# Decoder layer on one core: the start of the cross-attention placed within the second half of the self-attention

## The reference

```python
x = x + attn(layernorm(x), w_q, w_kv, w_dense)      # causal, 16 heads, 4 groups, head size 128
x = x + xattn(layernorm(x), ctx, mask, mask, Wq, bq, Wk, bk, Wv, bv)
x = x + ffn(layernorm(x), Wg, W1, W2, W3, bias)      # 8 experts, top 2

def xattn(target, source, target_mask, source_mask, ...):   # 16 heads of size 16, positions along the last axis (512)
    q = einsum('oc,bct->bot', Wq, target) + bq              # k, v from source in the same way
    dot = einsum('bhdt,bhds->bhts', q, k) / 4
    mask = target_mask[..., None] * source_mask[:, :, None, :]
    dot = mask * dot - (1 - mask) * 1e6
    amap = softmax(dot) * mask
    return einsum('bhts,bhds->bhdt', amap, v)
```

## Time and profile before

| | us |
|---|---|
| median of 3 runs | 2808.98 |
| lowest and highest | 2804.44, 2813.34 |
| the profiled execution, its time | 2802.59 |
| the profiled execution, its span | 2801.0 |
| PE busy in the span | 2603.9 (93%) |
| DVE busy | 1875.0 (67%) |
| ACT busy | 1455.1 (52%) |
| POOL busy | 995.5 (36%) |

### The profile page before, as it was taken

One profiled execution on the slowest core, in us unless ns is written; L12 is line 12 of the kernel. 1 busy time (PEld: TensorE's weight loads), 2 busy tenths in 40 slices (PEclk: granted clock), 3 DMA queues, 4 the chain that ended last, 5 costly groups with the idle time before them and its releaser, 6 DMA issues. The chain is left out here.

```text
span 2801.0 us, 51111 instructions
## 1 busy us (share of the span) xinstructions
PE 2603.9 (93%) x15536; PEld 1816.8 (65%) x15537; DVE 1875.0 (67%) x3845; ACT 1455.1 (52%) x2868; POOL 995.5 (36%) x1178
## 2 busy tenths in 40 slices
PE   7999999999999999999759999999999986399997
PEld 6888888888888888888524444444443423277775
DVE  6556655566544455554569898889888876576665
ACT  4334433345433344333337777777777765255554
POOL 1112211112111112211235665665665647433332
PEclk9999999999999999999879999999999988699999
DMA  4102222013201111111154555555655558655554
GB/s 150 69 7 75 75 75 75 26 49 136 91 31 61 45 45 60 60 47 43 53 123 118 133 136 136 139 131 136 139 135 130 133 147 287 230 101 106 111 106 83
DMA packets 140817, 282.49 MB, mean 101 GB/s; under 512 B 39344, under 2 KB 42288, under 8 KB 135616
## 3 DMA queue, kind: packets, MB, share of 16 engines
q1 hardware_dynamic: 112416, 214.99, 26.7%
q0 software_dynamic: 23664, 58.09, 10.0%
q10 hardware_dynamic: 4656, 8.40, 1.0%
HBM read 147.82 MB, written 81.68 MB: 82 GB/s over the span
## 5 line engine op out<-in xcount | busy, mean ns | idle before, releaser
L1566 DVE TENSOR_REDUCE b_negmax<-b_ps_s 128x2 f32<-128x1024 f32 x512 | 611.2, 1218 | 52.9 <-PE b_ps_s L1751 46.4
L278 POOL TENSOR_SCALAR probs<-probs,rinv 128x256 f32<-128x256 f32 x256 | 242.0, 945 | 1094.3 <-DVE rinv L435 1094.3
L1366 ACT ACTIVATE b_probs<-b_ps_s 128x1024 f32<-128x1024 f32 x512 | 520.0, 1020 | 198.9 <-PE b_ps_s L1762 197.6
L312 ACT ACTIVATE probs<-ps_s,negmax 128x128 f32<-128x128 f32 x256 | 94.1, 367 | 484.5 <-DVE negmax L428 484.5
L1775 PE MATMUL b_ps_o<-b_probs,b_v_stack 128*32 128x256 f32 (+1 forms) x2816 | 295.0, 491 | 0.9 <-ACT b_probs L1366 0.8
L1762 PEld LDWEIGHTS b_ps_s<-b_stack 56*128 56x128 f32 x1024 | 96.3, 184 | 272.4 <-issue 165.7
L1762 PE MATMUL b_ps_s<-b_stack 56*128 56x512 f32 x1024 | 257.6, 500 | 15.4 <-DVE b_negmax L1566 7.5
L1751 PE MATMUL b_ps_s<-b_stack 54*128 54x512 f32 x1024 | 228.7, 443 | 42.4 <-DMA b_stack<-b_split 24.0
L543 PE MATMUL ps_proj<-xT_h,wq_h 128*128 128x512 f32 x512 | 216.0, 422 | 0.0
L2461 POOL DMA_INDIRECT out<-e_y,e_place_int x71 | 118.1, 1664 | 253.4 <-DMA out<-e_y,e_place_int 218.4
L543 PE MATMUL ps_proj<-xT_h,wq_l 128*128 128x512 f32 x512 | 201.7, 394 | 0.0
(11 more groups left out here) (334 smaller groups left out, 6641.1 us busy)
## 6 DMA issues: line engine op xcount, KB each, us to landing
b_stack<-b_split SPq DMA_DIRECT2D x336, 128.0 KB
e_row<-rows_by_expert SPq DMA_DIRECT2D x71, 258.0 KB, 2.9
b_out_tiles<-row_sum_inverses SPq DMA_DIRECT2D x64, 256.0 KB
x<-acc SPq DMA_DIRECT2D x15, 1024.0 KB, 4.8
x_in<-in_x SPq DMA_DIRECT2D x8, 1024.0 KB, 8.1
normalised_x_split<-xT_h SPq DMA_DIRECT2D x8, 1024.0 KB, 9.8
normalised_x_split<-xT_l SPq DMA_DIRECT2D x8, 1024.0 KB, 11.0
acc<-in_x SPq DMA_DIRECT2D x8, 1024.0 KB, 11.3
```

What stands on the lines that cost most here:

```text
L278: nc.gpsimd.tensor_scalar(probs[:, s, P:3 * P], probs[:, s, P:3 * P], rinv[:, s, 1:2], None, ALU.mult).then_inc(probs_done, 1)
L312: nc.scalar.activation(probs[:, s, 0:P], ps_s[s][:, 0:P], ACT.Exp, bias=negmax[:, s, 0:1], accum_out=rowsum[:, s, 0:1])
L1366: nc.scalar.activation(probs[:, k % 2, p, :, :], ps[:], ACT.Exp, scale=0.25).then_inc(e_done, 1)
L1566: nc.vector.tensor_reduce(negmax[:, k, p, :], ps[:], AX.X, ALU.max, negate=True).then_inc(m_reduced, 1)
```

## The change

A new function `cross_preparation` allocates the cross-attention's weights, biases, `x_in`, `c_in`, `xn`, their splits and the small tensors at the addresses where they lie in the second phase, and returns one function per engine; `attention_phase` calls their parts. Its own tensors are laid out in another order, so that what lies under the prepared ones is not used any more at the time.

- SyncE: at the beginning of t = 8 it loads the mask cut into 128 rows of 64, the three weights and the biases; at the end of t = 8 it stores the mask rows in 32 transfers; at the beginning of t = 15 it loads sequence 0 (`x_in`, `c_in`, `mask_b`).
- GpSimd: `ident` and `minus_half` at the start; at t = 8, after each of the units 0 to 11, one step of the mask rows, now on 128 partitions; at t = 15 scale and shift after unit 6, and both low parts at the end.
- ScalarE, t = 15: high parts of the weights after units 1, 3, 5, normalised input after unit 8, its high part after unit 10, the context's high part after unit 14.
- VectorE, t = 15: low parts of the weights after units 2, 4, 6, statistics after unit 5. Its mask row operations are gone.
- The block of the self-attention doesn't wait for the last stores; SyncE waits for them before the first stack transfer, ScalarE before its first exponential.
- The cross-attention's block begins with the projections. SyncE issues the mask rows of quads 0 to 2 and sequence 1's load first, then waits for the tiles.

```diff
@@ attention_phase, sync @@
                 def body(t, kind, half):
+                    if kind == "fresh":
+                        load_weights_of_cross()
+                    if kind == "last":
+                        sp.wait_ge(proj_filled, FILLS * t + KT + G + 2)
+                        load_first_sequence()
...
+                    if kind == "fresh":
+                        store_mask_rows()
                 pairs(body)(sp)
-                sp.wait_ge(stored, 16 * (HALVES * PAIRS + TB))
@@ gpsimd @@
+                constants_of_cross()
...
+                        if kind == "fresh":
+                            mask_rows_step(u)
+                        if kind == "last" and u == TB + 2:
+                            norm_scale_of_cross()
+                    if kind == "last":
+                        pool.wait_ge(proj_filled, FILLS * (t + 1))
+                        lows_of_cross()
@@ scalar @@
+                        if last and u in (1, 3, 5):
+                            weight_high("kqv"[u // 2])
+                        if last and u == 8:
+                            first_normalised()
+                        if last and u == 10:
+                            first_x_high()
+                        if last and u == UNITS - 2:
+                            act.wait_ge(proj_filled, FILLS * (t + 1))
+                            first_context_high()
@@ vector @@
+                        if last and u in (2, 4, 6):
+                            weight_low("kqv"[u // 2 - 1])
+                        if last and u == 5:
+                            first_stats()
@@ cross_preparation (new) @@
+        def load_weights_of_cross():
+            sp.dma_start(mask_cut[:], mask.rearrange("b (c t) -> (b c) t", t=COLS)).then_inc(mask_loaded, 16)
+            for n, src in (("k", w_kT), ("q", w_qT), ("v", w_vT)):
+                sp.dma_start(w_stage[:, W_AT[n], :, :], src.rearrange("(k p) o -> p k o", p=P)).then_inc(w_loaded[n], 16)
+            load_bias("k", b_k)
+            load_bias("q", b_q)
+            sp.dma_start(bias_v[:], b_v.to_broadcast([P, C])).then_inc(bias_loaded["v"], 16)
+
+        def store_mask_rows():
+            sp.wait_ge(aux_step, AUX_STEPS)
+            for r in range(AUXROWS):
+                for side in range(2):
+                    for p in range(2):
+                        sp.dma_start(aux_dram[:, r, side, p, :].rearrange("b (c t) -> b c t", t=COLS), aux[:, r, side, :]).then_inc(aux_stored, 16)
...
+        def mask_rows_step(u):
+            if u == 0:
+                pool.wait_ge(mask_loaded, 16)
+                nc.gpsimd.memset(aux[:, AUXROWS - 2:AUXROWS, :, :], 1.0).then_inc(aux_step, 1)
+            if u == 1:
+                nc.gpsimd.tensor_scalar(one_minus[:], mask_cut[:], -1.0, 1.0, ALU.mult, ALU.add).then_inc(aux_step, 1)
+                pool.wait_ge(aux_step, 2)
...
+        def weight_high(name):
+            act.wait_ge(w_loaded[name], 16)
+            if name == "k":
+                act.wait_ge(aux_stored, 16 * 4 * AUXROWS)
...
+        def first_stats():
+            dve.wait_ge(xc_loaded, 32)
...
@@ cross_attention_phase, sync @@
-                sp.dma_start(mask_rows, mask).then_inc(mrow_loaded, 16)
-                load_weight("k", w_kT)
-                load_xc(0)
...
-                sp.wait_ge(aux_step, AUX_STEPS)
-                for p in range(2):
-                    sp.dma_start(aux_dram[:, 0:MASKROWS, :, p, :], aux).then_inc(aux_stored, 16)
-                    sp.dma_start(aux_dram[:, MASKROWS:AUXROWS, :, p, :], max_rows).then_inc(aux_stored, 16)
-                sp.wait_ge(aux_stored, 64)
+                sp.wait_ge(aux_stored, 16 * 4 * AUXROWS)
+                for q in range(QUADS - 1):
+                    stack_aux(0, q)
                 sp.wait_ge(xs_low, 1)
                 sp.wait_ge(cs_low, 1)
                 load_xc(1)
+                load_mask_col(0)
+                load_mask_r(0)
+                sp.wait_ge(x1_stored, 16 * X1_STORES)
                 sp.wait_ge(tile_low, 4)
-                stack_quad(0, 0)
-                stack_quad(0, 1)
+                stack_half(0, 0, 0, sp)
+                for i in range(2):
+                    stack_half(0, 1, i, sp)
```

More of the change, by code:

```diff
@@ L106, in attention_phase @@
         acc_loaded = sem("acc_loaded")
-        stored = sem("stored")
+        stored = ready["x1_stored"]
         stats_done = sem("stats_done")
@@ L721, in cross_attention_phase @@
+def cross_attention_phase(nc, x1_seq, context_seq, mask, mask_cols, aux_dram, rinv_dram, x2_seq, ready, tensors, prepared, prepared_small, W_PARTS, X1_STORES, route, size):
     B, C, T = x1_seq.shape
@@ L969, in stack_half @@
                                   half_stacked if (q, i) == (0, 1) else stacked[q], 16)
-        def load_bias(eng, n, src):
-            with nc.allow_non_contiguous_dma(reason="a small vector"):
-                heads = src.rearrange("(u d p i) h -> h u i d p", u=2, d=DH, p=2, i=2)
-                for q in range(QUADS):
-                    for i in range(2):
-                        eng.dma_start(bias[n][spread(q, i), :], heads[q // 2, q % 2, i]).then_inc(bias_loaded[n], 16)
-        W_AT = {"k": 0, "q": 1, "v": 2}
-        W_PARTS = {"k": 1, "q": 2, "v": 3}
         FIRST_BANKS = {"k0": ps_p[:], "k1": ps_s[0][:, 0, :], "q0": ps_s[0][:, 1, :], "q1": ps_s[1][:, 0, :],
@@ L2681, in decoder_layer, with cross @@
     xT_pairs = nc.dram_tensor("normalised_x_split", [B * S // BANK, 2, P, H // P, BANK], F32, kind="Internal").ap()
[L2682 to L2687 removed]
+    with ExitStack() as ctx:
+        ready, tensors, prepared, prepared_small, w_parts, prepare = cross_preparation(nc, ctx, x1, context, mask, x_wq, x_bq, x_wk, x_bk, x_wv, x_bv, aux)
+        attention_phase(nc, by_512(x), a_wq, a_wkv, a_wd, xT_pairs, by_512(x1), B * S, H, S, HEADS, GROUPS, ready, prepare)
+        x1_stores = 2 * (B * S // BANK) + BANK // P
+        def cross(route, size):
+            cross_attention_phase(nc, x1, context, mask, mask_cols, aux, rinv, x2, ready, tensors, prepared, prepared_small, w_parts, x1_stores, route, size)
+        context_and_experts_phase(nc, out, cross, f_wg, f_w13, f_w2, f_bias, *experts_scratch(nc))
 def kernel(**inputs):
```

343 lines of the change are left out of this document (194 added, 149 removed).

## The result

| | before | changed |
|---|---|---|
| median us | 2810.47 (4 runs, 2804.44 to 2813.34) | 2785.53 (4 runs, 2782.78 to 2786.92) |
| ratio, 95% interval | 1 | 0.9913 [0.9894, 0.9932] |
| the profiled execution, time and span | 2802.59, 2801.0 | 2785.0, 2783.5 |

The change saves 24.9 us of the median, 0.9%. A second comparison gave 2815.14 against 2787.72, 0.9911 [0.9878, 0.9944], so 27.4 us. The forecast was -26.7 us and 2782 us.

A forecast was written before the change was run, and what follows sets the result against it. TensorE's standstill at the handover was the limit, the phases otherwise keeping it supplied. Handover -32.5, t = 8 +1.3, last pair +4.5 give -26.7 us: 2782 against the median, range 2772 to 2796.

The forecast's parts named there:

- Step 1: Self-attention block's end: without the wait for the last store it ends at about 1374.9 against 1376.74, 1.8 us.
- The stack's landing: Handover: stack transfers took 6.1 us here, 3.9 in the next sequence; landing taken as 1391.0, bounds 1389.1 to 1391.3.
- Rival (d): Handover: DMA engines limit the starting stack transfers, shift only 20 us; -14 us, 2795, chance 0.06.
- I take 0, since the next item delays ScalarE by more than what is missing: t = 8: late dense weights stall ScalarE 0 to 2.7 us, taken as 0 because the mask's wait delays it more.
- cannot pass: t = 8: by ring order the mask's load stays behind the 1 MB store, so TensorE loses 1.3 us.
- Rival (e): After t = 8: 32 mask row stores block SyncE's queue; 83 us lost against 27 won, about 2865, chance 0.04.
- Last pair: Pair before the handover: added VectorE work costs 3.5 us and GpSimd's 1 us, sum 4.5, bounds 0 and 9.
- the lead of 1.3 us: Last pair: unit 3's probabilities are ready 1.3 us before being transposed, covering that much of VectorE's 4.8 us.
- each stall is at most 1.6 us: Last pair: added pieces are smaller and spread, so no TensorE stall exceeds 1.6 us and the clock may hold.
- rival (b): Last pair or mask's wait costs more, TensorE stalls over 2 us drop the clock; -17 to -22, about 2790, chance 0.14.
- GpSimd's low parts also move as a block and stay ahead of their readers: After the handover: sequence 1's low parts shift earlier with its other preparation and delay nothing; no cost entered.
- Rival (a): The forecast itself, whole kernel: -22 to -31 us, chance 0.62.

The follow-up runs named there:

- the run with all three improvements: Changed kernel with loads in t = 7 behind the accumulator's, GpSimd's low parts first, VectorE's additions behind its last unit; 2788.62 us, ratio 0.9890 to the kernel before.

## Why the prediction was right, and where its steps were not

**Handover: right in size, its parts less so.** 32.8 us against 32.5. Tiles ready 6.83 us after the first one, as taken over from the earlier trace rows. Step 1 was valued at 1.8 us; put back, the wait costs 3.3, since behind the longer pause TensorE's granted clock fell to 0.50 within the projections. The stack's landing was taken near the slower row, and it took 6.9 us. Rival (d), transfers limited by the DMA engines, did not happen in the changed kernel, but in the run in which VectorE takes two of the low parts the tiles were early and the product was not, so there the transfers bound what is left.

**t = 8: sum too small by 0.8 us, and the causes weighed wrongly.** Forecast +1.3, measured +2.14 and +2.04. The failing step is "I take 0, since the next item delays ScalarE by more than what is missing": the dense weights' lateness is 1.4 of the 2.0 us and the mask's wait 0.5 to 0.6. The mask's load, issued 0.42 us behind the 1 MB store, came 4.4 us later, at 728.2; the store had landed 4.7 us after its own issue, at 728.0. The Trainium skill (DMA: Bandwidth & Descriptors, Queues, rings and completion order) says that a DMA engine takes the descriptors of a ring in order, and the trace agrees; it also says that a later one may finish its write before an earlier one, so the forecast's "cannot pass" is more than the page states.

**Mask rows' stores: right.** The 32 issues took 22.62 us from 813.44, 0.7 us each, and t = 9 is no longer than before (82.75 us, where it was 83.06). Rival (e), 2865 us, is excluded.

**Last pair: the engine right, the sum right by luck.** Forecast +4.5, measured 4.7 in the first trace. But it was 3.5 for VectorE and 1 for GpSimd. GpSimd cost nothing that shows: no split was lengthened (1.26, 1.27 and 0.68 us), and scaling after scaling waits for VectorE, the one behind the normalisation too. VectorE's 4.7 us of work cost all they last, so the lead of 1.3 us saved nothing. The two errors cancel. The bound "each stall is at most 1.6 us" failed: one was 2.06 us, behind the statistics, though the clock stayed at 1.00 behind it, other than rival (b) has it for a stall over 2 us. Over all eight traces with these additions in the units, the pair took 64.4 to 67.0 us, 65.6 in the mean, so 5.8 us above before; five of them show a granted clock of 0.71 to 0.89 from 1370 to 1380 us, behind waits of 1.17 and 1.41 us that before has too. In the four variants with splits or all additions moved behind the last unit none does. That the additions make the fall likelier is what these counts suggest, not more. That VectorE gains no new lead from unit to unit is borne out: eight small pieces cost the same as four larger ones.

**After the handover: a step that was wrong.** "GpSimd's low parts also move as a block and stay ahead of their readers": they stay ahead of their readers, but they didn't move with the scores. GpSimd's low part of the input came 7.4 us later against the first product than before and fell on VectorE's copy of the maxima, 1.29 us instead of 0.18. The stretch grew by 0.9 to 1.3 us in the two traces of the changed kernel. With another order on GpSimd it is 27.68 to 28.18 us in four variants, against 28.61 to 29.77 in the traces with the old order and 27.70 before.

**Against the median.** -32.8 + 2.1 + 4.7 + 0.9 and +0.7 in other stretches of the attention part is -24.4 by the first pair of traces, without the sequences and the end. The medians say -24.9 and -27.4. Rival (a) it was. That 2782 is so near to 2785.5 is partly luck: the forecast had nothing for 0.9 us behind the handover and 0.8 us too little at t = 8, its two errors in the last pair cancel, and the conversion from trace to median was taken from one execution, 6.4 us below the median.

**Open.** From the last sequence's load to the end, the two traces of before take 653.1 and 653.5 us; the changed kernel and ten variants take 654.4 to 667.4. The code there is the same. Within it falls the start of the routing, where waits for transfers and for ScalarE (0.9 us in one trace, 15.0 in another) trade places. Both traces of before are of executions below its medians (2802.59 and 2805.91 us against 2810.47 to 2819.95), which speaks for luck. Whether the change costs some 3 us there, or before was lucky twice, these runs don't settle; nor whether the meetings of `b_r_out`, of which before shows none in two traces, became more frequent.

## To carry to other kernels

Work that is moved off a serial stretch is best put where its engine isn't part of a circle that sets the pace: here in the waits of 2 us at the tail, and a low busy share was no sign of such a place. Where engines turn at one pace, cutting the work into pieces saved nothing. Tiny transfers cost their issue time (0.64 us each here) to whatever is queued behind them, so they belong into a stretch in which the queue is idle. A wait at a block's end can cost more than it lasts, 3.3 us for 1.7 here.

## What the runs showed of the hardware

- An operation on 128x16 elements took 1.57 to 2.39 instead of 0.17 us when GpSimd's subtraction of 2.38 us had begun 0.02 to 0.85 us before it: `b_r_out` at 1524.65 ended with `p_x_l`, and in the run with all three improvements the value split took 2.51 instead of 0.68 us behind such a subtraction. The Trainium skill (SBUF — State Buffer, SBUF: two separate sides) states this as an exclusive lock for the whole instruction, against VectorE operations with two SBUF inputs; the traces agree. I had cited it for the splits in the last pair, where it cost nothing, and missed the place where some 0.1 us of timing decides on a wait of TensorE of 1.8 us.
- The same waits of TensorE (1.17 and 1.41 us) were followed by a granted clock of 1.00 in one trace and 0.71 in the next of the same kernel, 2.5 us apart.
- Transfers issued 0.6 us sooner landed 0.8 us later, in one trace: with the tiles early, the stack took 8.2 us instead of 6.9.
